# Image 15's channel means taken from sums of y, its squares by quarters, and the last inner stores split, in a two-stage normalise, convolve and attend kernel

## What is computed

```python
x = x + _L0_conv_ref(_gn(x), ...)     # per-image 5x5 and dilated 3x3 taps, then a 256 x 128 fusion
x = x + _L1_conv_ref(_gn(x), ...)     # halo attention, blocks of 8 x 8 with a halo of 4

def _gn(v, G=32, eps=1e-05):          # group normalisation, 8 channels to a group
    g = v.reshape(B_, G, C_ // G, H_, W_)
    m = jnp.mean(g, axis=(2, 3, 4), keepdims=True)
    s = jnp.var(g, axis=(2, 3, 4), keepdims=True)
    return ((g - m) / jnp.sqrt(s + eps)).reshape(v.shape)

# first layer, its end: y has 128 channels (two kinds of 64)
out = jnp.einsum('nchw,oc->nohw', y, fuse_w[:, :, 0, 0]) + fuse_b[None, :, None, None]

# attention: the mask leaves only keys outside the image
mask = jnp.broadcast_to(mpatch[None, :, None, None, :], (b, nb, heads, 1, K * K))
sim = jnp.where(mask, neg, sim)       # mpatch is true inside the image
attn = jax.nn.softmax(sim, axis=-1)
```

## Time and profile before

| | before |
|---|---|
| median of 3 runs | 225.84 us (225.5 to 227.42) |
| the profiled execution's own time | 225.6 us |
| its span in the profile | 223.8 us |
| mean granted TensorE clock | 0.98 of 2.4 GHz |
| busy, share of the span: PE | 188.3 us, 84% |
| DVE | 138.9 us, 62% |
| ACT | 134.8 us, 60% |
| POOL | 91.6 us, 41% |
| moved by DMA | 57.06 MB, mean 255 GB/s |

### The profile page before, as it was taken

One profiled execution on the slowest core, in us unless ns is written; L12 is line 12 of the kernel. 1 busy time (PEld: TensorE's weight loads), 2 busy tenths in 40 slices (PEclk: granted clock), 3 DMA queues, 4 the chain that ended last, 5 costly groups with the idle time before them and its releaser, 6 DMA issues.

```text
span 223.8 us, 3513 instructions
## 1 busy us (share of the span) xinstructions
PE 188.3 (84%) x1116; PEld 69.0 (31%) x1116; DVE 138.9 (62%) x338; ACT 134.8 (60%) x228; POOL 91.6 (41%) x203
## 2 busy tenths in 40 slices
PE   0003999799999999999999999999999999999440
PEld 0003243325323323233342333334333244334130
DVE  0487768956025866546665855867558675587932
ACT  0395779891324685909566595683955857559710
POOL 2005050524722513132396742359475139904331
PEclk9999999999999999999999999999999999999965
DMA  6999999995835769546867899799798898992705
GB/s 213 411 410 410 408 409 409 405 265 127 226 95 156 196 194 267 157 116 187 261 183 256 234 294 295 221 303 272 219 294 260 281 271 260 319 351 98 254 27 187
DMA packets 30802, 57.06 MB, mean 255 GB/s; under 512 B 3264, under 2 KB 12224, under 8 KB 30784
## 3 DMA queue, kind: packets, MB, share of 16 engines
q1 hardware_dynamic: 30400, 56.55, 78.8%
q10 hardware_dynamic: 384, 0.29, 0.4%
HBM read 17.85 MB, written 16.78 MB: 155 GB/s over the span
## 4 chain that ended last, share of the span: by engine, by line
PE 73%; DMA 9%; SPq 6%; DVE 4%; POOL 3%; ACT 2%; issue 1%; DVEq 0%; ACTq 0%; POOLq 0%
PE py L818 37%; PE pf L849 25%; DMA xs<-x_dram 9%; SPq L262 6%; PE pf L764 3%; PE py L866 3%; PE py L764 2%; DVE gs L560 2%; ACT junk L529 2%; POOL gs L353 1%; PE pf L778 1%; DVE xs L254 1%; POOL chain L400 0%; POOL chain L438 0%; POOL y L363 0%
## 5 line engine op out<-in xcount | busy, mean ns | idle before, releaser
L818 PE MATMUL py<-gs,wd 80*32 80x512 f32 x768 | 86.1, 594 | 0.0
L529 ACT ACTIVATE junk<-xs,nwb 128x1024 bf16<-128x1024 f32 x63 | 72.3, 1148 | 4.0 <-DVE xs L655 1.5
L655 DVE SCALAR_TENSOR_TENSOR xs<-pf,cst,xs 128x512 f32<-128x512 f32 x64 | 48.1, 751 | 21.0 <-PE pf L849 16.0
L849 PE MATMUL pf<-y,fw 128*128 128x512 f32 x128 | 59.1, 604 | 0.0
L509 ACT ACTIVATE y<-py,cst 128x512 f32<-128x512 f32 x32 | 20.3, 684 | 54.5 <-PE pf L849 49.6
L381 POOL TENSOR_TENSOR wd<-vals,cst 80x384 f32<-80x384 f32 x30 | 25.2, 844 | 56.2 <-PE py L818 55.9
L664 DVE SCALAR_TENSOR_TENSOR y<-py,cst,y 128x512 f32<-128x512 f32 x32 | 22.6, 747 | 35.1 <-PE py L818 35.0
L818 PEld LDWEIGHTS py<-gs,wd 80*32 80x32 f32 x768 | 23.1, 109 | 57.2 <-issue 56.5
L849 PEld LDWEIGHTS pf<-y,fw 128*128 128x128 f32 x128 | 23.0, 190 | 33.0 <-issue 33.0
L560 DVE BATCH_NORM_STATS2 gs<-xs 128x6 f32<-128x512 f32 x40 | 25.0, 681 | 12.0 <-DMA xs<-x_dram 11.9
L458 ACT ACTIVATE wd<-xs 128x1024 bf16<-128x1024 f32 x24 | 25.0, 1044 | 4.2 <-DMA xs<-x_dram 4.2
(11 more groups left out here) (84 smaller groups left out, 88.6 us busy)
## 6 DMA issues: line engine op xcount, KB each, us to landing
gs<-fc SPq DMA_DIRECT2D x128, 169.4 KB, 3.0
xs<-x_dram SPq DMA_DIRECT2D x15, 1024.0 KB, 18.8
out_dram<-xs SPq DMA_DIRECT2D x32, 256.0 KB, 3.1
out_dram<-xs SPq DMA_DIRECT2D x16, 512.0 KB, 3.9
xs<-x_dram SPq DMA_DIRECT2D x2, 512.0 KB, 17.3
gs<-wkv_dram SPq DMA_DIRECT2D x1, 256.0 KB, 15.5
gs<-wout_t_dram SPq DMA_DIRECT2D x1, 256.0 KB, 15.5
fw<-fusion_dram SPq DMA_DIRECT2D x1, 256.0 KB, 10.5
```

The source lines that it names most:

```text
L529: act.activation(junk[:, :], x1(n, c), func, scale=scale, bias=bias[:, c:c + 1], accum_out=acc[:, n, c, e:e + 1]).then_inc(s_stat, 1)
L655: dve.scalar_tensor_tensor(out=rows[:, t], in0=image(pf[:, bank * HALF:(bank + 1) * HALF]), scalar=fb[:, c:c + 1], in1=rows[:, t], op0=ALU ...
L818: mm = pe.matmul(py[n % 2][quad(q), s * HALF:(s + 1) * HALF], wd[0:KP, w0:w0 + QUAD], rows, start=(j == 0), stop=(j == PASSES - 1))
L849: pe.matmul(pf[:, bank * HALF:(bank + 1) * HALF], fw[:, t * C + 128 * c:t * C + 128 * (c + 1)], y[:, t * HALF:(t + 1) * HALF], start=True, ...
```

## The change

Three things change, all for the last chain.

1. The sums of image 15's x1 over its pixels are no longer taken from x1. The sum of x1 is the sum of x, plus the fusion weights times the sum of y, plus the biases. DVE reduces `y` of image 15 to `ysum` [128 x 2] right behind its last merge, and PE multiplies it by the fusion weights (four products of one column) behind `fuse(15)` into a free place of `py1`. `xmean`, the part that doesn't depend on y, is made once near the start. `last_mean` on DVE adds the two, behind the residual of image 15. DVE's `channel_sum` and ACT's sum over tile 0 go.
2. ACT squares image 15 in four quarters of 512 pixels, one behind each residual bank, in place of two passes over 1024. The second quarter of each channel tile goes to a column of a new tile `acc2`, zero elsewhere, which the group product adds in PSUM with a second small product.
3. DVE adds the vectors channel tile by channel tile, and SP stores images 15 and 14's inner rows as four DMAs of 256 KB in the order (15,0), (14,0), (15,1), (14,1), in place of two of 512 KB.

A memset of `acc2` on POOL is added at the start, and SP and ACT wait for it with the others (`s_zero` 4 in place of 3).

```diff
-STATS = [4 * (n + 1) for n in range(N - 1)] + [4 * N - 1]
+STATS = [4 * (n + 1) for n in range(N)]
...
             def inner(n):
-                if n < N - 1:
-                    sp.wait_ge(s_inner, n + 1)
-                if n >= N - 2:
-                    sp.wait_ge(s_innerd, N - n)
+                sp.wait_ge(s_inner, n + 1)
                 store_rows(n, IN0, IN1)
...
             outer(N - 1)
-            inner(N - 1)
-            inner(N - 2)
-            sp.wait_ge(s_store, 16 * 3 * N)
+            for n, c, done, count in ((N - 1, 0, s_innerd, 1), (N - 2, 0, s_inner, N - 1), (N - 1, 1, s_innerd, 2),
+                                      (N - 2, 1, s_innerd, 3)):
+                sp.wait_ge(done, count)
+                sp.dma_start(out_v[:, n * NC2 + c, IN0 * W:IN1 * W], x1(n, c)[:, IN0 * W:IN1 * W]).then_inc(s_store, 16)
+            sp.wait_ge(s_store, 16 * (3 * N + 2))
...
+            pool.memset(acc2[:, :], 0.0).then_inc(s_zero, 1)
...
-            statistics(N - 1, 0)
-            statistics(N - 1, 1, (1,))
+            for i, (c, t) in enumerate(bank_order(N - 1)):
+                act.wait_ge(s_res, 4 * (N - 1) + i + 1)
+                act.wait_ge(s_stat, 4 * (N - 1) + i)
+                act.activation(image(junk[:, 0:HALF]), by_parity(x1(N - 1, c))[:, t], ACT.Square,
+                               scale=KEYS * HW ** -0.5, bias=nwb2[:, c:c + 1],
+                               accum_out=acc2[:, 5 + 2 * c:6 + 2 * c] if t else acc[:, N - 1, c, 1:2]).then_inc(s_stat, 1)
...
-            def channel_sum(n, c):
-                dve.wait_ge(s_res, 4 * n + 4)
-                link(dve.reduce_sum(msum[:, :], x1(n, c), AX.X))
-                dve.tensor_scalar(acc[:, n, c, 0:1], msum[:, :], KEYS / HW, wbk[:, c:c + 1], ALU.mult,
-                                  ALU.subtract).then_inc(s_statd, 1)
+            def last_mean():
+                dve.wait_ge(s_ymean, 1)
+                dve.scalar_tensor_tensor(out=acc[:, N - 1, :, 0], in0=small(FINAL)[:, 32:32 + NC2], scalar=KEYS / HW,
+                                         in1=xmean[:, :], op0=ALU.mult, op1=ALU.add).then_inc(s_statd, 1)
...
+            dve.wait_ge(s_xs, 6 * BATCHES)
+            link(dve.tensor_tensor(xmean[:, :], mv[:, N - 1, :, 0], fb, ALU.add))
+            dve.scalar_tensor_tensor(out=xmean[:, :], in0=xmean[:, :], scalar=float(KEYS), in1=wbk[:, :],
+                                     op0=ALU.mult, op1=ALU.subtract)
...
                     merge(n + 1)
+                    dve.wait_ge(s_y, 2 * N)
+                    dve.reduce_sum(ysum[:, :], y.rearrange("p (t f) -> p t f", t=2), AX.X).then_inc(s_ysum, 1)
...
-            channel_sum(N - 1, 1)
+            last_mean()
...
-            add_inner(dve, N - 1).then_inc(s_innerd, 1)
-            add_inner(dve, N - 2, (1,)).then_inc(s_innerd, 1)
+            for n, c in ((N - 1, 0), (N - 1, 1), (N - 2, 1)):
+                add_inner(dve, n, (c,)).then_inc(s_innerd, 1)
...
-                pe.matmul(small(b)[:, 0:4 * size], gmat, acc[:, first_:first_ + size].rearrange("p j c s -> p (j c s)"),
-                          start=True, stop=True).then_inc(s_grp, 1)
+                mm = pe.matmul(small(b)[:, 0:4 * size], gmat, acc[:, first_:first_ + size].rearrange("p j c s -> p (j c s)"),
+                               start=True, stop=b < FINAL)
+                if b == FINAL:
+                    mm = pe.matmul(small(b)[:, 0:4 * size], gmat, acc2[:, :], start=False, stop=True)
+                mm.then_inc(s_grp, 1)
...
             fuse(N - 1)
+            pe.wait_ge(s_ysum, 1)
+            for c in range(NC2):
+                for t in range(2):
+                    mm = pe.matmul(small(FINAL)[:, 32 + c:33 + c], fw[:, t * C + 128 * c:t * C + 128 * (c + 1)],
+                                   ysum[:, t:t + 1], start=(t == 0), stop=(t == 1))
+            mm.then_inc(s_ymean, 1)
             group_product(FINAL)
```

More of the change, by code:

```diff
@@ L109, in build @@
         acc = sb("acc", [128, N, NC2, 2])
+        acc2 = sb("acc2", [128, 8])
+        ysum = sb("ysum", [128, 2])
+        xmean = sb("xmean", [128, NC2])
         blk = sb("blk", [128, N * NC2, 3, 3])
         minus_half = sb("minus_half", [128, NC2 * BATCH])
-        msum = sb("msum", [128, 1])
         at = sb("at", [128, NC2 * C])
@@ L169, in build @@
         s_stat = sem("x1_statistic_done")
-        s_statd = sem("x1_statistic_done_by_vector")
+        s_statd = sem("last_x1_mean_done_by_vector")
+        s_ysum = sem("last_y_sums_ready")
+        s_ymean = sem("last_fused_sums_done")
         s_blk = sem("block_sums_ready")
@@ L269, in _ @@
                          wout_t.rearrange("(k p) o -> p k o", p=128)).then_inc(s_attw, 16)
-            sp.wait_ge(s_zero, 3)
+            sp.wait_ge(s_zero, 4)
             def copies(h):
@@ L475, in _ @@
             act.wait_ge(s_const, 32)
-            act.wait_ge(s_zero, 3)
+            act.wait_ge(s_zero, 4)
             def x_sums(n):
@@ L518, in _, with statistics @@
             stats = [0]
-            def statistics(n, c, es=(0, 1)):
-                act.wait_ge(s_res, 4 * n + (2 * c + 2 if n < N - 1 else c + 3))
+            def statistics(n, c):
+                act.wait_ge(s_res, 4 * n + 2 * c + 2)
                 kinds = ((ACT.Identity, KEYS / HW, nwb1), (ACT.Square, KEYS * HW ** -0.5, nwb2))
-                for e in es:
-                    func, scale, bias = kinds[e]
+                for e, (func, scale, bias) in enumerate(kinds):
                     m = stats[0]
```

## The result

The change takes 223.68 us in the median of 14 runs (222.96 to 225.33), the kernel before 227.07 us of 14 (225.49 to 227.42); the ratio is 0.988, with a 95% interval of 0.9856 to 0.9905. The profiled executions took 223.27 and 225.6 us, 2.33 us apart. The times of each kernel fall into a lower and an upper group (before 6 of 14 at 225.5 to 225.9 and 8 at 226.9 to 227.4, after 10 at 223.0 to 224.3 and 4 at 224.8 to 225.3), and between like groups the medians differ by 2.3 us (225.65 and 223.4, 227.26 and 224.99), as the two profiles do, while the medians of all 14 differ by 3.4.

What follows compares the result with a forecast made beforehand. The prediction took the tail's chain of waits, with ACT's squares one behind the other, as the bound. -1.36 - 0.17 - 0.55 = -2.1 us on 225.6 gave 223.5, put at 223.6 us for the median; range 222.5 to 225.0.

Steps and rivals of the forecast that it cites:

- signs of being wrong: Profile signs against the forecast: group product ending after block sums, fourth residual late, or engines idle between the small stores.
- Up to the variance: Tail on ACT, PE and DVE: variance starts at 212.4 in place of 213.76, block sums last, -1.36 us.
- -1.4 us is all that DVE's list allows: Lower bound on the variance term: DVE's remaining operations permit no more than -1.4 us.
- A quarter of the squares: ACT's passes of 512 for image 15: about 0.83 us each, four ending at 211.4 in place of 213.3.
- The reduction of y under PE's cover: DVE's 1.22 us reduction is hidden while the fourth residual waits for PE; anything over 0.45 us longer comes through.
- The attention's clock: Last attention on PE: starts earlier, clock falls at 214.6 again, so 0.2 us run at full speed, -0.17 us.
- The rival of the full clock: Last attention wholly at full clock, -0.86 us in place of -0.17, giving 222.8 us; chance 0.24.
- The stores: Last four stores on SP: first issue 0.6 us earlier, DMA engines' bytes bound the end, -0.55 us.
- The rival of small stores: Small last stores cost what they gain: fourth lands at the median, +0.25 in place of -0.55, 224.3 us; chance 0.12.
- Slower by SP's queue: Last store issues on SP take up to 1.32 us each, fourth lands at 225.1, total 226.3 us; chance 0.06.
- Late mean: Mean from y on DVE's path comes 0.85 us later if its products run at half clock, 224.4 us; chance 0.08.
- The chances: Whole kernel against a 1% line: faster 0.44, within 1% 0.53, slower by over 1% 0.03; forecast itself 0.50.

Runs made afterwards that it cites:

- e5: The change with DVE's reduction of y made twice, 1.22 us more ahead of the last residual: 224.91 us in one execution.
- e4: The change plus products nobody reads on PE, one before the group product and two before the last attention: median 222.53 us of 6 runs, ratio to before 0.982.
- e6: The change with each of the last four stores cut in two of 128 KB: span ends 6.6 us after the last vectors' copy, in place of 5.44.
- e3: The change with ACT squaring image 15 in two passes of 1024 and one group product, mean still from y: ratio to before 0.9881.
- e3b: The kernel of e3 profiled in another execution: less a 1.60 us shift, the variance starts at 212.59, 0.44 us later than in the change.
- e10: The change with three products nobody reads in PE's gaps at 37 to 42 us: two of 6 runs at 225.03 and 225.04 us.

## Why the prediction was right, point by point

It said 223.6 us in 222.5 to 225.0, and 223.68 was measured; against the profiled execution of before the sum was -2.08 us and the profile gives -2.31. The mechanism is the predicted one in its main line, an earlier variance and earlier stores, but one of the prediction's signs of being wrong came true.

- **Up to the variance: predicted -1.36, measured -1.61.** 0.12 of it is upstream (merges ended at 205.76 against 205.88), 1.49 is the change. The step that was off is which input is last. The prediction had the block sums last, ending at 212.35, and the group product 0.3 us ahead, and named a group product that ends after the block sums as a sign of being wrong. It ends 0.23 us after them, at 212.12, and the variance starts 0.26 us after them: ACT decides still. The block sums end 1.43 us earlier, at 211.89, in place of 0.97, and of the wait for PE, which was to vanish, 0.26 of 0.44 us stay. The one-column products were sized right (0.95 us, predicted 1.03) but start under the last fusion product, at 209.19, and `last_mean` starts 0.04 us behind the residual; so the block sums begin 0.11 us behind the residual, not 0.43. That -1.4 us is all that DVE's list allows was wrong too, for the same reason.
- **A quarter of the squares: predicted 0.83 us, measured 0.91.** The pass is 0.72 us, not the 0.68 of the row taken, and 0.18 us lie between. The row taken was of an operation that reads PSUM (`pf`), while the quarters read `xs` in SBUF. The fixed part of a pass, counted from rows that both read SBUF, is thus 0.29 us (2 x 0.72 - 1.15) in place of 0.2. The first quarter began 0.2 us earlier than worked out, so the squares ended at 211.46 for 211.4: two errors that cancel.
- **The reduction of y under PE's cover: right for the residual, not for the squares.** The fourth residual started at 209.39, paced by PE, and e5 finds 0.4 us of slack there, predicted 0.45. But the squares hang on the first residual, and e5's went 1.1 us later for 1.22 us more on DVE. What made the reduction free is that the first residual started only 0.07 us later than before (207.01 and 206.94), since there it had waited 0.79 us for PE, and that ACT was still at image 14 until 207.83. POOL's eight adds moved by 0.94 us and held up nothing; the two operations for `xmean` lie in idle time of DVE (65.18 to 65.53, the residual starts at 67.27).
- **The attention's clock: predicted -0.17, measured 0.** The moment of the fall was taken from one execution, and an uncommon one. Its mean clock is 0.980; of 15 other executions of before with clocks on record and times under 226.3 us 13 have 0.972 to 0.974. If all their time at half clock lies in the tail, that is a fall near 212 (an estimate: 224.0 - 2 x 0.027 x 224.0 = 211.9; the same sum gives 214.8 for the profile of before, where 214.6 was read, and 212.2 for the change, where it was 212.35). The rival of the full clock didn't come true in the profile, but e4 shows that its price, 0.86 us predicted, is 0.83. By the same estimate it came true in part in one of the change's 14 executions: the fastest, 222.96 us with a mean clock of 0.985, fell near 214.6.
- **The stores: predicted -0.55, measured -0.70.** 0.61 is the earlier first issue; the rest goes with 379 GB/s in place of 360. The rival of small stores was wrong for 256 KB and right for eight of 128 KB. The Trainium skill, page "DMA: Bandwidth & Descriptors", Rules for kernel authors, says to coalesce many small transfers into a large one. Here only e6 bears that out, with 1.2 us lost; two of 512 KB were slower than four of 256.
- **Slower by SP's queue: no.** The issues took 0.345 to 0.455 us.
- **Late mean: no**, and e3 and e3b say that part 1, with the mean from y, is where most of the 1.5 us comes from.

That 223.6 stands 0.1 us from the median is luck in part, and in two ways. The terms were off by 0.25, 0.17 and 0.15 us, and not all one way. And the number was counted from 225.84, the median of three executions, while 14 gave 227.07: the medians fell by 3.4 us and not by 2.2, since 8 of 14 executions of before lie in the upper group, and only 4 of the change's. Like against like it is 2.3 us. The chances stood on the line of 1%, and so does the result: 2.3 us of 225.6 is 1.0%, the ratio says 1.2%.

## What to carry to other kernels

When one engine's work on the finished result is last, look for the same quantity one step upstream: a sum over a linear product is the product of a sum, and could be taken here while the large product still ran. Cut a last store only until a piece takes as long as its issue. Small products behind a dense phase may run at half clock, and a few products that nobody reads, in gaps that are idle anyhow, can buy that back: here 0.83 us of a last attention of 1.89. And when work is slipped in ahead of several followers, look at the slack of the first of them as well as of the last: the residual had 0.4 us, the squares 0.1.

## What the runs showed that I had not expected

- The same program has executions with a stretch at half clock (43.3 to 46.7 us) and without, behind gaps of 0.4 to 1.2 us and not behind a long idle stretch. It costs 1.5 to 1.7 us, more than half of what this change brought, and makes most of the spread of the times.
- With one group of gaps filled a fall can still come behind the next: 52.4 us in e10. Whether it moved there, or would have come there anyhow, one profile doesn't show.
- In e3, and in e6 too, such a stretch lay over the last fusion products, four products taking 5.4 us in place of 3.7.
